# Moving the copy, the turn and the turned maxima to other steps of a softmax group's pipeline

## What is computed

```python
q, k, v = (proj(Wq), proj(Wk), proj(Wv))
q = q * cos + _rotate_half(q) * sin
k = k * cos + _rotate_half(k) * sin
att = jnp.einsum('bhqd,bhkd->bhqk', q, k) / math.sqrt(hd)
att = jax.nn.softmax(att + mask, axis=-1)        # mask: causal
out = jnp.einsum('bhqk,bhkd->bhqd', att, v)
return out @ Wo.T
```

## Time and profile before

| | us |
|---|---|
| three runs of the kernel | 1095.83, 1096.02, 1099.04 |
| median | 1096.02 |
| the profiled execution | 1099.39 |
| its span, first to last instruction | 1097.6 |
| PE busy | 1049.9 (96%) |
| ACT, DVE, POOL busy | 618.4, 594.3, 489.9 |

### The profile page before, as it was taken

One profiled execution on the slowest core, in us unless ns is written; L12 is line 12 of the kernel. 1 busy time (PEld: TensorE's weight loads), 2 busy tenths in 40 slices (PEclk: granted clock), 3 DMA queues, 4 the chain that ended last, 5 costly groups with the idle time before them and its releaser, 6 DMA issues. The chain is left out here.

```text
span 1097.6 us, 33513 instructions
## 1 busy us (share of the span) xinstructions
PE 1049.9 (96%) x14381; PEld 828.6 (75%) x14384; DVE 594.3 (54%) x1326; ACT 618.4 (56%) x1172; POOL 489.9 (45%) x524
## 2 busy tenths in 40 slices
PE   4999999999999999999999899978899999999998
PEld 4888888888888888898888778856444444445787
DVE  6243434334243545545452763588778878785533
ACT  4544444444444555555554656675477777767763
POOL 1454455454454555554553534754133332221346
PEclk9999999999999999999999989998999999999999
DMA  3100101001001012102004120057522223200001
GB/s 135 57 3 3 57 3 36 24 3 50 17 2 50 17 31 72 32 17 86 17 23 140 41 68 1 1 129 212 113 53 53 55 46 59 60 3 2 1 20 58
DMA packets 19613, 50.77 MB, mean 46 GB/s; under 512 B 2687, under 2 KB 13759, under 8 KB 16575
## 3 DMA queue, kind: packets, MB, share of 16 engines
q1 hardware_dynamic: 19470, 48.67, 16.1%
HBM read 37.71 MB, written 10.75 MB: 44 GB/s over the span
## 5 line engine op out<-in xcount | busy, mean ns | idle before, releaser
L1893 DVE TENSOR_REDUCE aa_mx<-aa_S 128x1 f32<-128x640 f32 (+1 forms) x192 | 173.3, 953 | 46.5 <-PE aa_S L1609 45.5
L512 DVE SCALAR_TENSOR_TENSOR la_y<-la_g,la_O 128x512 f32<-128x512 f32 x64 | 41.1, 684 | 239.6 <-PE la_O L692 239.6
L1799 ACT ACTIVATE aa_PT<-keep 128x512 f32<-128x512 f32 (+1 forms) x203 | 110.6, 583 | 44.0 <-PE keep L1633 42.7
L602 PE MATMUL la_R<-a_hTh,WF 128*128 128x512 f32 x384 | 128.4, 400 | 4.2 <-DVE a_hTl L160 4.2
L1533 POOL TENSOR_SCALAR_AFFINE_SELECT aa_PT<-aa_PT 128x256 f32<-128x256 f32 (+1 forms) x112 | 49.5, 442 | 177.8 <-ACT aa_PT L1799 174.6
L298 POOL TENSOR_TENSOR la_qd<-q,la_C 128x512 f32<-128x512 f32 x64 | 81.2, 1290 | 95.2 <-PE la_O L692 95.2
L311 POOL TENSOR_TENSOR la_yl<-la_y,la_yh 128x512 fp32r<-128x512 f32 x62 | 79.2, 1301 | 89.3 <-ACT la_yh L392 89.3
L361 ACT ACTIVATE q<-la_R 128x512 f32<-128x512 f32 x64 | 38.4, 599 | 117.0 <-PE la_R L602 117.0
L519 DVE TENSOR_TENSOR X<-la_R,X 128x512 f32<-128x512 f32 x64 | 44.3, 692 | 94.2 <-PE la_R L602 94.1
L1077 POOL TENSOR_TENSOR f_fl<-f_f,f_fh 128x512 fp32r<-128x512 f32 x48 | 61.8, 1296 | 65.1 <-ACT f_fh L936 65.0
L319 POOL TENSOR_TENSOR fin_sqacc<-fin_sqacc,la_sq 128x512 f32<-128x512 f32 x64 | 86.3, 1349 | 7.9 <-DVE X L1199 3.3
(11 more groups left out here) (288 smaller groups left out, 2782.9 us busy)
## 6 DMA issues: line engine op xcount, KB each, us to landing
la_Wraw<-w_quads_dram SPq DMA_DIRECT2D x7, 1280.0 KB, 5.5
aa_stacks<-k_parts SPq DMA_DIRECT2D x16, 256.0 KB, 6.6
q_parts<-aa_QP SPq DMA_DIRECT2D x8, 384.0 KB, 4.8
aa_stacks<-q_parts SPq DMA_DIRECT2D x8, 384.0 KB, 4.8
k_parts<-aa_KP SPq DMA_DIRECT2D x8, 384.0 KB, 4.3
qw_w<-w_ffn_dram SPq DMA_DIRECT2D x12, 192.0 KB, 2.4
q_ffn<-qw_w SPq DMA_DIRECT2D x12, 192.0 KB, 1.9
X<-hidden_dram SPq DMA_DIRECT2D x4, 512.0 KB, 7.3
```

The source lines that it names most:

```text
L602: m = pe.matmul(out, a, b, start=n == 0, stop=n == len(pairs) - 1)
L1799: act.activation(PT[:, (NM2 * g + b) % NPT, h:h + nh, 0:w], ST[at % NB][:, 0:nh * w].rearrange("p (h q) -> p h q", h=nh), ACT.Exp, scale=S ...
L1893: dve.reduce_max(out, src, AXX).then_inc(s1_free, 1)
```

## The change

Three numbers of the order are changed. The last half of a group's outputs is copied behind the exponential of step 8 instead of 4, and turned and normalised at the end of step 9 instead of 7. The first half of the next group's maxima is turned, copied and sent by DMA ahead of step 23 instead of 17 (24 instead of 18 in group 0); the second half and all `parts` stay where they are.

```diff
-        N_T1, N_T0 = LAST[1], LAST[5]
+        N_T1, N_T0 = LAST[2], LAST[5]
...
                 need = g * NST + (FIRST[4] if h else FIRST[0])
-                row = min(done + 8, need - 3)
+                row = min(done + (8 if h else 14), need - (3 if h else 8))
                 part = min(done + 3, row - 1)
...
-                    if n == FIRST[1] and g >= 1:
+                    if n == FIRST[2] and g >= 1:
                         outputs(g - 1, 1)
```

## The result

The changed kernel takes 1108.63 us in the median of four runs (1108.42 to 1108.80), the kernel before 1097.07 (1095.83 to 1099.04, four runs): a ratio of 1.0103, with an interval of 1.0091 to 1.0116. Measured again beside 17 runs of the kernel before it was 1.0101 (1.0075 to 1.0127). So it is slower by some 11 us. I had forecast 1103.9 with a range up to 1108.0: the sign was right, the loss was a third too small, and the time lies outside the range. Two things lie behind that: the second part of the change cost 1.3 us more than I had summed, and 1.57 us come from a stretch of half clock that my sum put at nothing.

The account below looks back on a forecast made before the run. PE was taken to set the pace of each group. Outputs 4.6, last group 1.2, DMA wait -0.4 and maxima 2.5 summed to 7.9 us over the median of 1096.02, giving 1103.9 us, range 1099.0 to 1108.0.

Parts of the forecast that it names:

- What bounds the kernel: A group of 28.54 us goes at the pace of PE, busy 27.81; only what holds up or spares PE moves time.
- Part 1, its size: Outputs' copy behind step 8, turn at the end of step 9: costs 0.77 us a group, 4.6 in groups 1 to 6.
- the bare wait ahead of step 8: PE at step 8 waits for the bank of step 5, formerly covered by the turn; recorded stall of some 0.25 expected.
- Part 1, its cause: At the end of step 9 the turn waits 0.66 us on PE for ACT's copy of the outputs.
- My first rival: Gain comes as meant: outputs' copy ends before PE reaches the turn, stalls at steps 7 and 18 spared; 1090.5 us, chance 0.06.
- Part 2, the gain ahead of step 22's values: First-half maxima no longer turned ahead of step 17: step 18's stall goes, values of step 22 start 0.16 us earlier.
- Part 2, what follows the values: Maxima turned ahead of step 23 delay ACT, stalling PE at steps 26, 28, 30; net cost with earlier gain 0.35 a group.
- The stall ahead of step 26: Step 26 waits for the bank of exponential 23, delayed by the maxima's copy: 0.31 us of new stall.
- The DMAs: The four moved DMAs of maxima are issued over 6 us before their reader, step 0 of the next group: no cost.
- The clock: Half clock after new stalls, perhaps near group 7's 1.3 us: costs 3.4, giving 1107.3 us or more; chance 0.07.
- the rival: The clock falls: half clock followed PE busy 1.45 of 3.40 us, full clock followed 2.07; 1107.3 us, chance 0.07.
- The sum: Whole kernel: 4.6 + 1.2 - 0.4 + 2.5 = 7.9 us slower, 1103.9 us against the median of 1096.02.

## Why the prediction was right or wrong

**What bounds the kernel.** Right. In every kernel tried, a group's length changed by what PE was held up or spared.

**Part 1, its size.** Right: 0.77 was forecast, 0.78 measured, in each of groups 1 to 6. The pieces hold as well: step 7 without its stall, the bare wait ahead of step 8 (873.89 - 873.48 = 0.41, where 873.48 is the start of step 7 and 0.17), the turn 0.05 after the end of the copy (874.95 + 0.63 = 875.58, turn at 875.63). The last group took 1.31 more in place of 1.2 (from its first exponential to its last, 31.77 before and 33.08 now). The one wait for the DMA of the maxima went, 0.39, as said. By the Trainium skill, "PSUM — Partial Sum Buffer", section "Engine vs sequencer instructions", matmuls keep their order; this case's trace agrees: step 10's product, whose bank was free, started at 876.13, 0.50 after the waiting turn.

**Part 1, its cause.** Half wrong. I wrote that PE waits for the copy, and gave the wait for DVE behind it as a small addition of 0.15. As an account of the changed kernel that holds (0.07 was left of the second wait). As a cause it doesn't: the runs showed that the first wait hides the second, and with the copy early DVE's wait alone costs as much. My first rival ("decides once ACT is 0.66 us nearer") was wrong for the same reason. An earlier copy would not have given the gain that it names; the run with the copy behind step 7 was 0.48 nearer and gained nothing at all.

**Part 2, the gain ahead of step 22's values.** Mis-sized: 0.16 forecast, 0.03 measured (from step 15 to these values 5.08 us, from 880.93 to 886.01, instead of the 5.11 of before). I took 0.06 between the end of DVE's maximum and the turn, a handover that I had read from ACT. Here DVE ends at 883.03 and the turn starts at 883.17, 0.14 later; and the turn then takes 0.46, where 0.44 was read from one whose weights were loaded ahead. It isn't that DVE hands over more slowly: step 10's segment starts 0.05 behind the maximum that it waited for (875.15 + 1.23 = 876.38, segment at 876.43). With DVE in turn waiting for this turn, the delay passes on.

**Part 2, what follows the values.** Mis-sized by less: the copy of the maxima and the wait behind it held ACT for 0.77 (888.30 to 889.07) where I had 0.72, and the stretch from the values of step 22 to those of step 30 took 6.27 us, where my steps gave 6.19. The stall ahead of step 26 is there as forecast. Together 0.55 a group instead of 0.35 (0.44 in group 0): 3.76 us instead of 2.5. This is 1.3 of the missing us. My own terms were also added up loosely: the shift of 0.06, the stalls of 0.31, 0.15 and 0.07, less 0.2, make 0.39 and not 0.35; and the low end of the whole took 0 for this part, where I had named -0.16 a group.

**The DMAs.** Right: no wait of PE for the moved ones, at either place.

**The clock.** The step that failed most. I gave the half clock a chance of 0.07, for stalls inside the groups, where it never came, and nothing in the sum. It came behind the loop, in a stretch that the change doesn't touch, and cost 1.57 us in the changed kernel's trace. I had also added my sum to the median as if half-clock stretches were a constant of the kernel. And the rival rested on a wrong reading. I wrote that behind the stretch with PE busy 1.45 of 3.40 us the clock was half. The row behind it says that it stayed at 1.00:

```profile
737.30:744.10 6.80, 6.80 (x34) 5.20 (x35) 6.55 (x8) 5.79 (x12) 6.30 (x6) 1.00 0.78 188
```

The row at 1016.50 above, with 1.46 of 3.40 and full clock behind it, is a second case. So the busy share of one such stretch doesn't tell in this trace whether the clock falls, and the rival rested on nothing that I had shown.

**The sum.** 9.35 for the loop and 1.57 behind it make 10.9, against 11.6 between the medians; the remaining 0.6 is within what the kernel before scatters from run to run. From my 1103.9 to the 1108.6 measured is 4.7: part 2 is 1.3 of it, part 1 with its last group 0.2, the half clock 1.6, those 0.6, and 1.0 is luck of the base, since the median of the kernel before came out at 1097.07 in four runs where I had added to the 1096.02 of three.

## What to carry to other kernels

When two waits stand one behind the other on the engine that sets the pace, the profile can show only the first, and removing it uncovers the other. Before a wait is called the price, ask what the next instruction waits for if it goes. In this kernel a long reduction in a ring of two banks wanted other work of TensorE behind it (the turn behind the value products cost 0.18 a group), not the next user of the ring (0.78); and a copy that ScalarE had to fit in belonged ahead of a long block of matmuls, not behind it (0.59 a group). A loop can be 1 us shorter and the kernel no faster, so compare the length of the loop in the trace and the time of the kernel separately.

## What the runs showed of the hardware

The same quiet stretch behind the loop (PE busy 7.77 of 10 us) runs at a mean granted clock of 1.00 in some kernels and 0.83 in others, the same in each trace of the two kernels that were traced again, and what lies behind the loop takes 1.4 to 1.7 us longer with it (83.75 to 83.90 against 82.23 and 82.31).

A turn of four transposes of 128 columns takes 0.50 us when its first weight load starts together with its first matmul: behind the wait for its copy (875.63 to 876.13), and also behind the value products in the kernel that turns at step 10, where it waited for nothing (873.40 to 873.90). It takes 0.44 where that load started 0.10 ahead (872.41 and 872.51).

In the changed kernel a matmul starts 0.05 us behind the end of what it waited for, on ACT (875.58 to 875.63) and on DVE (876.38 to 876.43). The turn of step 18 started 0.14 behind DVE (883.03 to 883.17). It waits for two semaphores, and in the trace a semaphore instruction of line 1657 stands at 883.1 between the end of the maximum and the weight load.
